# Shifted-window attention on one core: value rows and outputs by transposes, products of 48 channels regrouped, and another order of the work on every engine

## What is computed

```python
h = _layer_norm(x, ln1_g, ln1_b)
h = jnp.roll(h, (-SHIFT, -SHIFT), axis=(1, 2))
xw = _window_partition(h, WS).reshape(-1, N, C)          # windows of 7 x 7 = 49 pixels
qkv = xw @ w_qkv + b_qkv
...
attn = jnp.einsum('whnd,whmd->whnm', q, k) + rel_bias + mask   # 6 heads of 8 channels
attn = jax.nn.softmax(attn, axis=-1)
o = jnp.einsum('whnm,whmd->whnd', attn, v)
o = o @ w_proj + b_proj
x = shortcut + o                                          # after windows and roll are undone
y = _layer_norm(x, ln2_g, ln2_b)
y = conv3x3(y, w_ffn1) * bn1_scale + bn1_shift            # zero padding of y
y = conv1x1(gelu(y), w_ffn2) * bn2_scale + bn2_shift
return x + y
```

## Time and profile before

| | |
|---|---|
| median of 3 runs | 3166.82 us |
| the three runs | 3130.7, 3166.82, 3233.46 us |
| profiled execution, its own time | 3155.91 us |
| its span, first to last instruction | 3154.1 us |
| `layer0` | from 0 to about 304 us of the span |
| `attention` | from about 304 to 2224 us |
| `feed_forward` | from about 2224 to 3154 us |
| busy over the span: TensorE / VectorE / ScalarE / POOL | 91% / 66% / 63% / 58% |

### The profile page before, as it was taken

How to read it: one execution, slowest core, us unless ns; L and a number is a source line. 1 busy time by engine, 2 the same in 40 slices (tenths; PEclk the granted TensorE clock), 3 DMA queues, 4 the chain that set the end, 5 groups by cost and what they waited for, 6 DMA issues and landing times. The chain is left out here.

```text
span 3154.1 us, 109482 instructions
## 1 busy us (share of the span) xinstructions
PE 2885.7 (91%) x42512; PEld 1858.9 (59%) x42512; DVE 2090.5 (66%) x3747; ACT 1992.5 (63%) x3766; POOL 1837.5 (58%) x2039
## 2 busy tenths in 40 slices
PE   7886999999999999999999999999499999999998
PEld 2332566666666666666666666665367676676665
DVE  1223577777777777766777777776366666666665
ACT  2443577777777777766777777876244444444444
POOL 0222577777777777755777777775255555555553
PEclk9998799999999999977999999999699999999999
DMA  5553111111111111111111111111888687877861
GB/s 133 148 146 89 27 43 42 42 42 42 42 42 42 42 42 42 42 38 32 42 42 42 42 43 42 44 42 37 143 132 134 113 138 120 135 130 119 134 104 32
DMA packets 235601, 231.29 MB, mean 73 GB/s; under 512 B 117808, under 2 KB 230448, under 8 KB 232368
## 3 DMA queue, kind: packets, MB, share of 16 engines
q1 hardware_dynamic: 235440, 229.05, 36.4%
HBM read 151.17 MB, written 77.76 MB: 73 GB/s over the span
## 5 line engine op out<-in xcount | busy, mean ns | idle before, releaser
L637 POOL TENSOR_TENSOR kex<-ks,cw 112x294 f32<-112x294 f32 x1024 | 775.8, 789 | 296.1 <-ACT ks L948 296.1
L736 PE MATMUL ps_t<-cw,s 113*98 113x113 f32 x3072 | 410.6, 271 | 102.5 <-ACT s L964 65.4
L736 PEld LDWEIGHTS ps_t<-cw,s 113*98 113x98 f32 x3072 | 296.0, 130 | 268.9 <-ACT s L964 158.9
L971 ACT ACTIVATE pt<-ps_t 98x588 f32<-98x588 f32 x512 | 335.6, 655 | 126.8 <-PE ps_t L736 123.2
L1103 DVE TENSOR_REDUCE mx<-s 113x12 f32<-113x588 f32 x512 | 392.2, 766 | 17.6
L1096 DVE TENSOR_TENSOR s<-ps_s,bias 113x588 f32<-113x588 f32 x512 | 391.5, 765 | 17.1 <-PE ps_s L724 12.8
L751 PEld LDWEIGHTS ps_o<-vs,pt 98*49 98x49 f32 x12288 | 309.6, 128 | 141.1 <-DVE on L1127 71.6
L724 PE MATMUL ps_s<-kex,q 48*49 48x294 f32 x4096 | 378.9, 433 | 1.4 <-issue 1.1
L1350 POOL TENSOR_TENSOR v<-ya 128x448 f32<-128x448 f32 x112 | 106.3, 949 | 452.2 <-PE ps_b L1396 427.7
L964 ACT ACTIVATE s<-s 113x588 f32<-113x588 f32 x512 | 348.3, 680 | 3.4 <-DVE s L1109 3.3
L631 POOL TENSOR_TENSOR s<-s,mx 113x588 f32<-113x588 f32 x256 | 300.6, 1174 | 68.7 <-DVE mx L1103 68.7
(11 more groups left out here) (149 smaller groups left out, 6097.2 us busy)
## 6 DMA issues: line engine op xcount, KB each, us to landing
ya<-y_chunks SPq DMA_DIRECT2D x64, 532.9 KB, 10.1
y_chunks<-y SPq DMA_DIRECT2D x256, 76.1 KB, 1.8
xin<-x_chunks SPq DMA_DIRECT2D x256, 73.5 KB, 2.5
xres<-x_chunks SPq DMA_DIRECT2D x256, 73.5 KB, 1.9
x_chunks<-xo SPq DMA_DIRECT2D x256, 73.5 KB, 1.8
out<-xr SPq DMA_DIRECT2D x32, 588.0 KB, 6.3
yb<-y_chunks SPq DMA_DIRECT2D x96, 177.6 KB, 6.3
xr<-x_chunks SPq DMA_DIRECT2D x32, 514.5 KB, 8.1
```

Source lines behind the costliest of these rows:

```text
L637: ins = pool.tensor_tensor(kex[a][:, win, :, :], ks[:, win, :].unsqueeze(1).to_broadcast([PP, HEADS, N]), w("head").unsqueeze(2).to_broadc ...
L736: mm = pe.transpose(ps_t[0:2 * N, i, j * 2 * BO:j * 2 * BO + QP], s_sb[d][:, i, part], w("ident"))
L971: act.activation(pt[d][:, :, :, :, :].rearrange("q i j u n -> q i (j u) n"), ps_t[0:2 * N, :, 0:HEADS * BO].rearrange("q i (g n) -> q i g ...
```

## The change

- `outputs` no longer multiplies by a selection matrix. `on` is laid out by duos, and four transposes against the identity give the channels of all 8 windows.
- The value rows are made in two steps. `values_and_projection` makes the values of a chunk as a straight product (channels by 392 pixels) into `ps_m`; ScalarE copies them twice side by side into the new tile `vc` (`value_channels`); TensorE turns each window with one transpose (8 of them). POOL's copy `twice` goes.
- The products are paired anew: queries (now crossed, which swaps the images) with the first variance; keys (crossed) with the second variance; values with the projection; the two centrings as before.
- The round is in another order on TensorE, ScalarE, VectorE and POOL. The layer norm of the input is one round further ahead (`n+3` is centred in round `n`), that of the output one round later. The rounds before the first chunk and after the last are made by the same `body`.
- The second layer norm's weight `g2` moves into the copy `xc2`, and its bias `be2` into the feed-forward's shift; the border of `y` holds minus the bias instead of zero. ScalarE's pass over `y` (L997) goes. `feed_forward` gets three sums over the bias at its start.

In all code below `has(n, k)` says whether chunk `n+k` exists.

```diff
@@ tensor: outputs
-                for win in range(NWC):
-                    for img in range(2):
-                        mm = pe.matmul(ps_k[BO * img:BO * img + C, win * N:(win + 1) * N], on[a][:, win, :],
-                                       w("pick")[:, img * N:(img + 1) * N], start=True, stop=True)
+                for d in range(DUOS):
+                    mm = pe.transpose(ps_k[0:PP, d * 2 * BO:d * 2 * BO + QP],
+                                      on[a][:, d, :, :].rearrange("q i c -> q (i c)")[:, 0:PP], w("ident"))
@@ tensor: pairs of products
+            def queries_and_variance(n):
+                if has(n, 1):
+                    pe.wait_ge(h_done, n + 2)
+                if has(n, 2):
+                    pe.wait_ge(xc_set, n + 3)
...
+                        mq = crossed(ps_m[:, 0, :], wqs, h, i)
+                        mv = straight(ps_m[:, 1, :], w("sum"), sq, i)
+            def keys_and_variance2(n):
...
+                        mk = crossed(ps_k, wks, h, i)
+                        m2 = straight(ps_m[:, 0, :], w("sum"), sq2, i)
+            def values_and_projection(n):
+                if has(n, 2):
+                    pe.wait_ge(ln_done, n + 3)
+                if has(n, 1):
+                    pe.wait_ge(k_set, n + 2)
+                if has(n, -2):
+                    pe.wait_ge(ot_set, n - 1)
...
+                        mv = straight(ps_m[:, 1, :], wvs, h, i)
+                        mp = crossed(ps_k, w("wp"), ot, i)
@@ tensor: value rows
+            def value_rows(n):
+                pe.wait_ge(vc_set, n + 1)
...
+                for win in range(NWC):
+                    mm = pe.transpose(ps_m[0:2 * N, win // 4, win % 4 * 2 * BO:win % 4 * 2 * BO + PP],
+                                      vc[:, win, :, :].rearrange("c s k -> c (s k)"), w("ident")[0:PP, 0:PP])
@@ tensor: the round
+                scores(n, 0, a); values(n - 1, 0, 1 - a)
+                scores(n, 1, a); queries_and_variance(n)
+                transposes(n - 1, 3); scores(n, 2, a)
+                keys_and_variance2(n); values(n - 1, 1, 1 - a)
+                values_and_projection(n); scores(n, 3, a)
+                transposes(n, 0); value_rows(n + 1)
+                transposes(n, 1); outputs(n - 1, 1 - a)
+                centers(n, a); transposes(n, 2)
@@ scalar
+            def value_channels(n):
+                act.wait_ge(v_mm, n + 1)
+                if has(n, -1):
+                    act.wait_ge(vt_mm, n)
+                act.activation(vc[:, :, :, :], ps_m[0:PP, 1, 0:T2].rearrange("c (w k) -> c w k", w=NWC).unsqueeze(2).to_broadcast(
+                    [PP, NWC, 2, N]), ACT.Copy).then_inc(vc_set, 1)
-                act.activation(xc2[:, :], ps_m[0:PP, 1, 0:T2], ACT.Copy)
-                act.activation(sq2[BO:PP, :], ps_m[0:C, 1, 0:T2], ACT.Square)
-                act.activation(sq2[0:C, :], ps_m[BO:PP, 1, 0:T2], ACT.Square).then_inc(squared2, 1)
+                act.activation(xc2[:, :], ps_m[0:PP, 1, 0:T2], ACT.Identity, scale=w("g2")).then_inc(xc2_set, 1)
+                act.activation(sq2[:, :], ps_m[0:PP, 1, 0:T2], ACT.Square).then_inc(squared2, 1)
-            def y_affine(n, a):
-                act.wait_ge(ymul_done, n + 1)
-                act.activation(y[a][:, :, 1:1 + W], y[a][:, :, 1:1 + W], ACT.Identity, bias=w("be2"),
-                               scale=w("g2")).then_inc(y_set, 1)
@@ gpsimd
-                pool.tensor_copy(h[:, :, 1, :], h[:, :, 0, :]).then_inc(h_twice, 1)
@@ feed_forward, gpsimd: border rows
+            pool.wait_ge(pad_ready, 1)
-                        ins = pool.memset(ya[b][:, a, row * YW:(row + 1) * YW], 0.0)
+                        ins = pool.tensor_copy(ya[b][:, a, row * YW:(row + 1) * YW], pad[:, 0:1].to_broadcast([128, YW]))
@@ feed_forward, vector
+            dve.wait_ge(weights_in, 16)
+            dve.tensor_scalar(pad[:, 0:1], w("be_a"), -1.0, None, op0=ALU.mult)
+            dve.tensor_scalar(pad[0:PP, 1:2], w("be_b"), -1.0, None, op0=ALU.mult).then_inc(pad_ready, 1)
```

506 lines of the change are left out of this document (237 added, 269 removed).

## The result

| | before | after |
|---|---|---|
| median of the runs (4 and 4) | 3152.11 us | 2849.32 us |
| their range | 3130.7 to 3233.46 | 2847.57 to 2854.49 |
| profiled execution | 3155.91, span 3154.1 | 2847.57, span 2845.8 |
| mean granted clock in it | 0.961 | 0.975 |
| one round, 900 to 1300 us | 14.30 us | 12.16 us |

The ratio is 0.906, with a 95% interval from 0.899 to 0.913. Ratios here leave out slow executions, those over 1.5% above the fastest of their kernel. The time is 71 us under the forecast of 2920 and 16 under the low end of the range, 2865. Faster by more than 2% came true; the size did not.

A forecast was written before the change was run, and what follows sets the result against it. TensorE was taken to set the pace: a round falls from 14.29 to 12.43 us, times 128 is 238 us; 3156 - 238 + 3 (attention's edges) + 4 (feed-forward's start) = 2925, forecast as 2920, range 2865 to 3000.

The forecast's parts named there:

- the half-clock stretch that I kept: Middle of attention: a half-clock stretch costing 30 us was expected again; 2895 us with none, 2925 with one.
- Value rows and outputs: TensorE: 8 transposes for value rows, 0.96 us (gain 0.56); 4 for outputs, 0.48 (gain 0.38).
- rival B: Transposes cost two passes or new waits take back most: round 13.87 us, 3109 us in all; chance 0.05.
- The spacings: TensorE's start-to-start times in the old round, laid end to end in the new order: 12.31 us against 14.17.
- The 0.12 called the loop's: Attention: the loop of two rounds adds 0.12 us on the mean, making the new round 12.43 us.
- The reserves: Three close places where TensorE needs ScalarE's results; each was forecast ready 0.2 to 0.4 us early.
- Rival A: The reserves don't hold, each late by 0.2 to 0.3: round 13.2 us, 3023 us in all; chance 0.12.
- (a): Queries wait for `xc`, ScalarE's last work of the round before: ready at 2.0 against 2.37, reserve 0.3 to 0.4 us.
- (b): The values-product waits for the keys' copy: ready at 6.3 against 6.50, reserve 0.2 us.
- (c): The value rows wait for ScalarE's new `vc`, 0.84 us long: ready at 8.25 against 8.57, reserve 0.3 us.
- rival C: Slower by the clock: a TensorE that never rests gets half clock for long stretches, over 3230 us; chance 0.03.
- The edges: Attention's filling and emptying +3 us, bounds -5 and +15; feed-forward's start +4, its first load waiting for the weights.

The follow-up runs named there:

- b_no_y_pass: The kernel before with ScalarE's pass over `y` (L997) left out; 3168.03 us, ratio 1.010.
- b_out_transposes: The kernel before with only its outputs made by 4 transposes in place of 16 products; 3399.74 us, ratio 1.085.
- a_vc_twice: The kernel after with ScalarE's copy of 784 columns made twice, first into a spare tile right in front of `vc`; 2941.08 us in one execution.

## Why the prediction missed, step by step

The forecast for the profiled execution was 2925; it took 2847.57. The 77 us between them: 36 in the round, 30 in the half-clock stretch that I kept, 3 in two short falls of the clock, and 8 at the edges. Two steps failed: the prices of the round, which I took from spacings that still held waits and changes of shape, and the stretch at half clock, which I kept because I read it as one that follows no idle time.

**The round: 12.43 forecast, 12.16 measured, 0.27 x 128 = 35 us (the 36 take the 14.30 of before instead of 14.29).**

*Value rows and outputs.* The rule "one record each, 0.12 us" held in kind: 8 and 4 records, so rival B fell. (What I called two passes are the two records that each other product leaves; the traces show no more than the records.) Its price was too high. The 0.12 came from six transposes at 0.69 to 0.73, which hold one change of shape of 0.10; without it a transpose is 0.10. The value rows were forecast at 0.96: they take 0.77 where nothing waits behind them, and 1.10 in the new round, 0.33 of it wait. The outputs were forecast at 0.48: they take 0.39 in front of whole-array work, and 0.60 in the new round, where the centrings behind them are of another shape and follow VectorE's copy. I had read no wait there.

*The spacings.* The step that failed is the table of spacings, which I applied with fixed prices: "transposes of six 0.69 to 0.73" and "a pair of quarter products ... 0.89 to transposes (1.19 less the 0.30 that it waited)". Two groups of six in front of full-height work took 0.63 (to the value rows) and 0.59 (to the outputs), 0.72 in the sum. The pair in front of transposes took 0.77 (1008.55 to 1009.32), not 0.89. So subtracting the named wait from a spacing left 0.12 of the wait in it. The group of value products without change of neighbours came out as forecast, 1.21. Over all groups the spacings add up to 0.15 less than forecast, with the 0.14 and 0.12 that value rows and outputs take more already counted against it.

*The 0.12 called the loop's.* The forecast set the round at 12.31 and added 0.12 for "the loop of two rounds". That step failed too: most of it was a third wait of TensorE. VectorE's and then TensorE's timeline of the kernel before show it, in the round of the earlier trace rows and in the next:

```profile
927.44 0.23 DVE L1141 SCALAR_TENSOR_TENSOR xo<-ps_m,bps,xres 112x21 f32<-112x21 f32 x1
...
941.86 0.23 DVE L1141 SCALAR_TENSOR_TENSOR xo<-ps_m,bps,xres 112x21 f32<-112x21 f32 x1
```

```profile
941.38 0.83 PE L703 MATMUL ps_k<-h,wks 48*64 48x392 f32 x4
942.35 0.51 PE L703 MATMUL ps_m<-xin,cw 48*64 48x392 f32 x1
```

The centrings start 0.48 behind the start of the residual's last piece in the one round (927.44 to 927.92) and 0.49 in the other, and the same in the two rounds after. They follow VectorE, not the keys in front of them: from the keys it is 0.78 in one round and 0.97 in the next. The list of TensorE's waits has only the two of the earlier trace rows; this one stands in no line with its releaser. It is 0.19 in every second round at least, so about 0.1 on the mean; TensorE waited about 1.0 us of a round and not the 0.90 that I read from two lines. In the new order the rounds are all alike, though the centrings follow VectorE in it too, now behind `vs`.

*The order.* "ScalarE is late there though it has time to spare ... a matter of order" is shown from both sides: ScalarE's work could be cut without gain, and moving one group of transposes back cost 1.26.

*The reserves.* Rival A fell. ScalarE's timeline after the change has the three ends (start, duration):

```profile
1001.33 0.83 ACT L933 ACTIVATE vc<-ps_m 112x784 f32<-112x784 f32 x1 [0.67 <-PE ps_m L691]
...
1007.58 0.51 ACT L902 ACTIVATE xc<-ps_m 112x392 f32<-112x392 f32 x1
...
1011.75 0.59 ACT L926 ACTIVATE ks<-ps_k,bks 112x392 f32<-112x392 f32 x1
```

(a) `xc` ends at 1008.09, the queries start at 1008.55: 0.46, forecast 0.3 to 0.4. (b) The keys' copy ends at 1012.34, the values-product starts at 1012.55: 0.21, forecast 0.2. (c) `vc` ends at 1002.16, the value rows start at 1002.33: 0.17, forecast 0.3. These distances are not all reserve: where a wait for ScalarE is named, TensorE starts 0.14 behind the end of its pass (`pt` after the change, and the value rows in the version with `vc` twice). That leaves 0.32, 0.07 and 0.03, so (b) and (c) were as good as used up. `vc` took 0.83, forecast 0.84. What the walk through the round missed is the `ps_t` wait in front of the second transposes, 0.17 as named (forecast none over 0.1), because the shorter value rows no longer cover ScalarE's copy, and the centrings' wait for `vs`.

*The load of the others.* VectorE came out at 11.22 as forecast, but not because it kept its work: its normalisation of `h` takes 1029 ns instead of 615, and denser work overlaps more. The prediction's reading that the subtraction is long where POOL is at work beside it is too simple: before the change POOL works beside all 56, and those beside the products for `kex` take 0.76, those beside `y` and the copy of `h` 1.0 to 1.2; after it, one beside `kex` takes 1.12 and one with POOL idle 0.76. ScalarE has 10.66 where I had 11.05. Back to back its passes start before the one ahead ends (0.59 long, next start 0.47 later in the rows around the keys' copy), so a denser round has less busy time than the sum of its passes; how much of the 0.4 that is, no run separates.

**The half clock: 30 us in the middle, 3 in two single rounds, and a part of the last rounds.** The step that failed is the reading in rival C: "The trace shows a stretch at half clock that follows no idle time: 94% busy, then 0.50". 94% was the mean over the window. TensorE's timeline at the start of that stretch shows the two waits of the round just in front of it:

```profile
1379.67 0.76 PE L736 MATMUL ps_t<-cw,s 113*98 113x113 f32 x6 [0.30 <-ACT pt L971]
...
1381.00 1.28 PE L751 MATMUL ps_o<-vs,pt 98*49 98x18 f32 x48
1382.81 1.37 PE L736 MATMUL ps_t<-cw,s 113*98 113x113 f32 x6 [0.52 <-ACT s L964]
```

Up to the values each group has its usual length; the six transposes behind the second wait take 1.37 instead of 0.79, so the clock fell from 2.4 to 1.2 GHz there. That these waits have to do with it is shown by the two filled versions: the same kernels with work in the waits have no such stretch between attention's first rounds and its last. Rival C had the sign wrong: the denser round did not lose the clock, it kept it: the trace of the kernel after has no such stretch, and its four executions have mean clocks of 0.969 to 0.975. Its counterpart, that the new round has no half clock and the time is 2895, stood in the prediction as what the Trainium skill (TensorE: Matmul & The Clock Gate, Part 1) would make of it, and I gave it no weight. By that rule, idle time lowers the clock and activity releases it; the filled versions agree with it in kind. The Trainium skill (TensorE: Matmul & The Clock Gate, A second HAM failure mode) also tells of a kernel whose short idle times between groups of products make the clock go to and fro, which is nearer to this case and which I did not weigh. With no stretch, and nothing else changed, the forecast would have been 2895, still 47 above the 2847.57.

The low end of the range fell with both steps: 2870 stood for no stretch and a round of 12.3, and I had let the round vary from there upwards only, as if the spacings read from the trace held no waits.

**The edges.** Attention's two ends were forecast at +3 together. The start came at +3.9 and the last rounds at -10.0, of which 2.1 are the 128th round; that makes -4, inside the bounds of -5 and +15. The feed-forward's start was forecast at +4 and came at +2.9 for the whole feed-forward. The queue of SP shows the first load of `ya` 6.5 us behind the weights' load, where it was 0.7:

```profile
1913.07 0.36 SPq L1238 DMA_DIRECT2D cw<-pack  x1
1919.59 0.34 SPq L1247 DMA_DIRECT2D ya<-y_chunks  x1
```

The load is later by more than the 4 I had worked out (5.8), and the whole stretch is longer by 2.9 only; what took up the rest, no run separates.

**What stays open.** Why a stretch begins in one round and not in the next, with the same waits in both, no run tells. Nor is it clear which waits bring one. The version with `vc` twice has one of 0.52 per round with one of 0.18 close behind it, and had no stretch in one execution. The version with the transposes moved back has one of 0.70 and two smaller ones, and had one short stretch. The version with outputs by transposes has 0.62 and 0.57, 3.2 us apart from start to start, and had nine. What VectorE's copy `vs` costs the new round was not tried either: no version makes it shorter or moves the centrings off its bank. A version that loads the feed-forward's first rows without waiting for all its weights was not tried. No version found beats the kernel after; the one with the outputs moved is its equal.

## What to carry to other kernels

Where the busiest engine waits for one that has idle time of its own, the gain is in the order and not in taking work off either: here the move of six transposes was worth 1.26 us of a round, while faster outputs or a shorter ScalarE in the old order gave 0.2 or less. Look at the granted clock wherever TensorE has short waits in every round, and where they can't be removed, try filling them: a few idle products cost nothing here, and by the medians won 2.5% in the kernel before and 9% in the version with outputs by transposes. Not every such wait costs the clock, as the version with `vc` twice shows. Price a group of products by what stands next to it (0.1 us for each change between the whole array and a part), and look for a start that follows another engine by the same distance in every round, which can be a wait though no list names it.

## What the runs showed of the hardware

- Kernels whose TensorE waited 0.30 and 0.52, or 0.62 and 0.57 us, in each round of 14 us had stretches of 27 to 99 us at half clock inside attention: one in `before`, one in `b_no_y_pass`, nine in `b_out_transposes` (3325 us). With the 0.52 filled, or with both of the longer ones, there were none, at 3124 and 3108 us. With one wait of 0.52 and one of 0.18 in a round of 12.87 (`a_vc_twice`) there was none either.
- The spread of one kernel's times went with its mean clock: 103 us before the change, 121 us over 13 runs on another chip (clock 0.970 at the fastest, 0.924 at the slowest), and 7 us for the kernel after, 14 and 29 for the filled ones.
- A change between products on the whole array and on a quarter of it cost 0.10 us each.
- An f32 transpose of 112 rows was one record, 0.10 us in a group of eight with nothing to wait for (0.77; eight more took 0.76); with a one-column product of the whole array between each two of them, that product cost 0.14 (0.41 for three).
- One VectorE instruction of one shape, the normalisation of `h`, took 615 ns on the mean before the change, 1029 after, 839 with a copy more on POOL and 553 with a row maximum more on VectorE. POOL was at work beside it both at 1029 and at 553, so what decides its length stays open. The copy on POOL changed the time by nothing that can be seen: 2850.33 against 2849.32.
- TensorE started 0.14 us behind the end of a ScalarE pass that it waited for (`after`, `a_vc_twice`), and 0.25 to 0.30 behind the end of VectorE's copy or residual (`before`, `after` and its variants).
